# A graph network on one core: GpSimd clears a tile between its scatters, VectorE keeps small operands in PSUM, ScalarE makes source one-hots before it waits for flips

## What is computed

```python
gate = silu(edge_attr @ F1W + F1b) @ F2W + F2b
gate = gate + (ei * (ej @ adapt)).sum(-1, keepdims=True)   # kinds of the edge's two nodes
msg = gate * h[dst] * (cw * mj)[:, None]
agg = segment_sum(msg, src, num_segments=N)
for i in range(4):                                          # attention
    score = (qi * kj).sum(-1) + 0.1 * (edge_attr * qi[:, :RBF]).sum(-1) + logm[dst]
    ...
for _ in range(5):                                          # spreading
    h = (1.0 - ALPHA) * segment_sum(w[:, None] * h[row], col, num_segments=n) + ALPHA * x
```

## Time and profile before

| | |
|---|---|
| median of 3 runs | 8893.94 us (8884.61 to 8922.17) |
| the profiled execution | 8923.99 us, its span 8922.2 us |
| TensorE busy | 6968.6 us (78%) |
| VectorE busy | 5923.4 us (66%) |
| ScalarE busy | 4708.0 us (53%) |
| GpSimd busy | 5514.9 us (62%) in 7877 instructions |
| mean granted clock of TensorE | 0.874 of full speed |

### The profile page before, as it was taken

One profiled execution on the slowest core, in us unless ns is written; L12 is line 12 of the kernel. 1 busy time (PEld: TensorE's weight loads), 2 busy tenths in 40 slices (PEclk: granted clock), 3 DMA queues, 4 the chain that ended last, 5 costly groups with the idle time before them and its releaser, 6 DMA issues. The chain is left out here.

```text
span 8922.2 us, 298973 instructions
## 1 busy us (share of the span) xinstructions
PE 6968.6 (78%) x145656; PEld 6141.4 (69%) x92274; DVE 5923.4 (66%) x15778; ACT 4708.0 (53%) x14842; POOL 5514.9 (62%) x7877
## 2 busy tenths in 40 slices
PE   5544445444545999999699989998999989997998
PEld 4433333333334989988488858886888778887998
DVE  5555555555555889988688868886788678873111
ACT  0222222222223777777488858886788768881000
POOL 2266666666665666666488858886788768880000
PEclk9866666666667999999799979998999889998999
DMA  9522222222223777777377737773677457764565
GB/s 391 205 73 74 76 78 74 74 77 77 76 76 114 242 249 243 247 243 243 107 234 234 233 102 231 237 233 115 225 235 234 161 175 234 237 196 190 242 254 209
DMA packets 735833, 1616.82 MB, mean 181 GB/s; under 512 B 97576, under 2 KB 427272, under 8 KB 729955
## 3 DMA queue, kind: packets, MB, share of 16 engines
q1 hardware_dynamic: 674798, 1514.15, 50.6%
q0 software_dynamic: 52768, 77.90, 2.7%
q10 hardware_dynamic: 6869, 5.50, 0.2%
HBM read 1177.09 MB, written 420.09 MB: 179 GB/s over the span
## 5 line engine op out<-in xcount | busy, mean ns | idle before, releaser
L2011 ACT ACTIVATE vals<-carry_h,weight 128x49 f32<-128x49 f32 x9604 | 2322.8, 328 | 6.5
L1012 POOL DMA_INDIRECT edge_records<-rec_space,slot_all x1600 | 1587.5, 992 | 1104.4 <-DVE slot_all L995 560.2
L436 PE MATMUL psum<-TT,hd_t 128*128 128x97 bf16 x9604 | 1379.2, 208 | 106.0 <-POOL ts L2127 69.1
L430 PE MATMUL psum<-TT,hd_t 128*128 128x97 bf16 x19208 | 1443.4, 208 | 0.0
L436 PEld LDWEIGHTS psum<-TT,hd_t 128*128 128x128 fp8e4 x9604 | 938.2, 98 | 404.2 <-DVE carry_h L2125 69.9
L2056 POOL TENSOR_TENSOR vals<-vals 128x343 f32<-128x343 f32 x1372 | 1077.7, 785 | 92.8
L2051 POOL TENSOR_TENSOR vals<-vals 128x343 f32<-128x343 f32 x1372 | 1045.1, 762 | 4.6 <-ACT vals L2011 4.6
L771 ACT COPY attr_t<-psum 80x500 f32<-80x500 f32 x200 | 114.4, 572 | 1629.0 <-remote 1406.6
L430 PE MATMUL psum<-ts,hs_t 128*128 128x49 bf16 x19208 | 921.5, 184 | 0.1
L1916 DVE SCALAR_TENSOR_TENSOR xks<-recs,psum 128x343 f32<-128x343 f32 x1372 | 695.3, 507 | 331.5 <-PE psum L430 324.0
L1888 PE MATMUL psum<-vals,hs 128*128 128x147 bf16 x9604 | 873.0, 234 | 24.0 <-POOL vals L2056 24.0
(11 more groups left out here) (361 smaller groups left out, 15618.2 us busy)
## 6 DMA issues: line engine op xcount, KB each, us to landing
AJ<-adjacency SPq DMA_DIRECT2D x35, 5488.0 KB, 16.8
recs<-attributes SPq DMA_DIRECT2D x196, 686.0 KB, 5.5
hs<-one_hots SPq DMA_DIRECT2D x392, 336.0 KB, 3.1
one_hots<-hots SPq DMA_DIRECT2D x343, 336.0 KB, 4.1
edge_records<-zeros SPq DMA_DIRECT2D x49, 2278.5 KB
recs_g<-edge_records SPq DMA_DIRECT2D x343, 325.5 KB, 5.1
recs<-attributes SPq DMA_DIRECT2D x196, 514.5 KB, 3.7
hd_t<-one_hots SPq DMA_DIRECT2D x196, 448.0 KB, 4.7
```

What stands on the lines that cost most here:

```text
L430: return e.add_instruction(mybir.InstMatmult(name=nc.get_next_instruction_name(), engine=mybir.EngineType.PE, ldweights=False, start_tenso ...
L436: e.matmul(out, hot, parts[0], start=True, stop=False)
L1012: e.indirect_dma_start(REC[:, :], bass.IndirectOffsetOnAxis(ap=slot_all[:, i % SR, s:s + 1], axis=0), rec_rings[:, (i // 2) % 4, s, i % 2, ...
L2011: last = e.activation(vals[:, c, 0, :], carry_h[:, par(back), c, :], ACT.Copy, scale=weight[:, par(back), c:c + 1])
```

## The change

- `pause`, a new tile of 128 x 8 floats: ahead of the 2nd to the 8th scatter of an iteration GpSimd clears it (`memset`), raises the new semaphore `s_pause` and waits for it before the scatter.
- `iota_ps` (iota for the one-hots), `own_keys` (the keys of 25 steps, copied anew every 25, `KEYED`), `rank`, `slot_m` and `over_b` (the result of L990, until now written over `slot_b`) lie in PSUM bank 4 beside the mask. `told` gives the values of `s_load`, which now has some more steps: the copy of iota, and the 8 copies of keys, each with a wait for VectorE's step before.
- ScalarE calls `mark_sources(i + 2)` ahead of `take(i + 4)`.
- The semaphore `k_flat` is merged into `s_kept`, so that waits for the key rows also await the kind table's store (counts go up by 18).

```diff
+KEYED = 25
 FIRST_LAID, LAID_GAP = 36, 3
...
-            rank = sb(st, "rank", [EP, 2, NS])
-            slot_a, slot_b, slot_m = (sb(st, n, [EP, NS]) for n in ("slot_a", "slot_b", "slot_m"))
+            slot_a, slot_b = (sb(st, n, [EP, NS]) for n in ("slot_a", "slot_b"))
+            pause = sb(st, "pause", [P, 8])
...
-                    e.wait_ge(k_flat, 1)
+                    e.wait_ge(s_kept, 1)
-                    e.copy(embT, bank(6)[0:G, 0:NELEM]).then_inc(k_flat, 1)
+                    e.copy(embT, bank(6)[0:G, 0:NELEM]).then_inc(s_kept, 1)
-                    e.copy(EMB[:, 0:G], bank(6)[0:NELEM, 0:G]).then_inc(k_flat, 1)
-                    e.wait_ge(k_flat, 2)
-                    e.dma_start(KINDS[:, :], EMB).then_inc(k_flat, 16)
+                    e.copy(EMB[:, 0:G], bank(6)[0:NELEM, 0:G]).then_inc(s_kept, 1)
+                    e.wait_ge(s_kept, 2)
+                    e.dma_start(KINDS[:, :], EMB).then_inc(s_kept, 16)
-                    e.wait_ge(k_flat, 18)
+                    e.wait_ge(s_kept, 19)
...
-                    e.wait_ge(s_kept, 1)
+                    e.wait_ge(s_kept, 19)
...
-                    e.wait_ge(s_kept, 1)
+                    e.wait_ge(s_kept, 19)
...
                 by_stream = lambda arr: arr[:, :].rearrange("p (s i) -> p s i", s=NS)
                 found_ps = bank(0, 2)
                 hist_ps = bank(3)[:, 0:8 * NB].rearrange("p (q s b) -> p q s b", q=4, s=2)
-                mask = bank(4)[0:EP, 0:EP]
+                mask, iota_ps = bank(4)[0:EP, 0:EP], bank(4)[0:EP, P:P + NB]
+                own_keys = bank(4)[0:EP, 192:192 + KEYED * NS].rearrange("p (s i) -> p s i", s=NS)
+                rank = bank(4)[0:EP, 400:400 + 2 * NS].rearrange("p (r s) -> p r s", r=2)
+                slot_m, over_b = bank(4)[0:EP, 432:432 + NS], bank(4)[0:EP, 448:448 + NS]
                 pair_of = lambda hots, i, q: hots[:, i % 3, 2 * q:2 * q + 2, :].rearrange("p s b -> p (s b)")
 
...
                     mark_sources(0)
                     mark_sources(1)
                     for i in range(ITER):
-                        mlp_step(i + LEAD, "take", READY)
                         if i + 2 < ITER:
                             mark_sources(i + 2)
+                        mlp_step(i + LEAD, "take", READY)
                         mlp_step(i + LEAD - 1, "activate", READY)
                         mlp_step(i + LEAD - 2, "assemble", READY)
 
                 if name == "vector":
-                    iota49 = iota_f[0:EP, 0:NB].unsqueeze(1).broadcast_to([EP, NS, NB])
+                    iota49 = iota_ps.unsqueeze(1).broadcast_to([EP, NS, NB])
 
                     def make_hots(i):
...
                         e.tensor_tensor(one_bd[:, i % 3], iota49, bdv, ALU.is_equal).then_inc(s_hot, 1)
 
                     def rank_stream(i, s):
+                        if s == 0 and i % KEYED == 0:
+                            e.tensor_copy(own_keys, by_stream(key_f)[:, :, i:i + KEYED]).then_inc(s_load, 1)
+                            e.wait_ge(s_load, told(i - 1, 0) if i else 3)
                         if s == 0 and i % KC == 0:
                             e.wait_ge(s_keys[i // KC % 2], 16 * (i // KC // 2 + 1))
                         o = (i % KC) * NS * EP + s * EP
-                        last = e.scalar_tensor_tensor(junk[:, s * EP:(s + 1) * EP], key_rows[:, i // KC % 2, o:o + EP], key_f[:, s * SC + i:s * SC + i + 1], mask,
+                        last = e.scalar_tensor_tensor(junk[:, s * EP:(s + 1) * EP], key_rows[:, i // KC % 2, o:o + EP], own_keys[:, s, i % KEYED:i % KEYED + 1], mask,
                                                       ALU.is_equal, ALU.mult, accum_out=rank[:, i % 2, s:s + 1])
                         if s == NS - 1:
                             last.then_inc(s_rank, 1)
 
+                    told = lambda i, n: 3 + 4 * i + min(i + 1, ITER - 1) // KEYED + n
                     e.tensor_copy(mask, lower[:, :]).then_inc(s_load, 1)
+                    e.tensor_copy(iota_ps, iota_f[0:EP, 0:NB]).then_inc(s_load, 1)
+                    e.wait_ge(s_load, 2)
                     make_hots(0)
                     make_hots(1)
...
                     for s in range(2):
                         e.tensor_copy(next_base[64 * s:64 * s + NB, :, s, 1, :], base[64 * s:64 * s + NB, :, s, 1, :])
                     move_on(0)
-                    e.wait_ge(s_load, 1)
                     for s in range(NS):
                         rank_stream(0, s)
...
                         e.wait_ge(s_looked, i + 1)
                         e.tensor_reduce(found[:, :, :], look[:, :, :, :], AX.X, ALU.add).then_inc(s_load, 1)
                         rank_more(2)
-                        e.wait_ge(s_load, 4 * i + 2)
-                        e.tensor_tensor(slot_m[:, :], rank[:, i % 2, :], found[:, :, 0], ALU.add).then_inc(s_load, 1)
+                        e.wait_ge(s_load, told(i, 1))
+                        e.tensor_tensor(slot_m, rank[:, i % 2, :], found[:, :, 0], ALU.add).then_inc(s_load, 1)
                         rank_more(1)
-                        e.wait_ge(s_load, 4 * i + 3)
-                        e.scalar_tensor_tensor(slot_a[:, :], slot_m[:, :], float(NB), home[:, i % 3, :], ALU.mult, ALU.add)
-                        e.scalar_tensor_tensor(slot_b[:, :], slot_m[:, :], float(1 - NB), found[:, :, 1], ALU.mult, ALU.add).then_inc(s_load, 1)
+                        e.wait_ge(s_load, told(i, 2))
+                        e.scalar_tensor_tensor(slot_a[:, :], slot_m, float(NB), home[:, i % 3, :], ALU.mult, ALU.add)
+                        e.scalar_tensor_tensor(slot_b[:, :], slot_m, float(1 - NB), found[:, :, 1], ALU.mult, ALU.add).then_inc(s_load, 1)
                         rank_more(1)
-                        e.wait_ge(s_load, 4 * i + 4)
-                        e.scalar_tensor_tensor(slot_b[:, :], slot_m[:, :], float(CAP), slot_b[:, :], ALU.is_ge, ALU.mult).then_inc(s_load, 1)
+                        e.wait_ge(s_load, told(i, 3))
+                        e.scalar_tensor_tensor(over_b, slot_m, float(CAP), slot_b[:, :], ALU.is_ge, ALU.mult).then_inc(s_load, 1)
                         rank_more(2)
                         if i >= SR:
                             scattered(i - SR)
-                        e.wait_ge(s_load, 4 * i + 5)
-                        e.tensor_tensor(slot_i[:, i % SR, :], slot_a[:, :], slot_b[:, :], ALU.add).then_inc(s_idx, 1)
+                        e.wait_ge(s_load, told(i, 4))
+                        e.tensor_tensor(slot_i[:, i % SR, :], slot_a[:, :], over_b, ALU.add).then_inc(s_idx, 1)
                         if i + 1 < ITER - 1:
                             move_on(i + 1)
...
                         if i >= 4:
                             scattered(i - 4)
                         for s in range(NS):
+                            if s:
+                                e.memset(pause[:, :], 0.0).then_inc(s_pause, 1)
+                                e.wait_ge(s_pause, i * (NS - 1) + s)
                             e.indirect_dma_start(REC[:, :], bass.IndirectOffsetOnAxis(ap=slot_all[:, i % SR, s:s + 1], axis=0),
                                                  rec_rings[:, (i // 2) % 4, s, i % 2, :], None).then_inc(s_scat[i % 4], 16)
                     for i in range(ITER - 4, ITER):
```

More of the change, by code:

```diff
@@ L80, in build @@
         s_flat, s_found, s_looked = sem("place_cells_counted"), sem("place_bases_found"), sem("place_bases_looked_up")
-        s_kept, s_keys = sem("rows_in_dram"), [sem(f"key_rows_loaded_{k}") for k in range(2)]
+        s_kept, s_keys = sem("kinds_and_rows_in_dram"), [sem(f"key_rows_loaded_{k}") for k in range(2)]
         s_srcrows = [sem(f"source_rows_loaded_{k}") for k in range(2)]
@@ L89, in build @@
         s_apes, s_afold = sem("adj_multiplied"), sem("adj_folded")
[L90 removed]
+        s_kinds, k_taken, k_row = (sem("kinds_" + n) for n in ("loaded", "taken", "in_rows"))
+        s_pause = sem("place_pause_over")
         s_mixed, s_high, s_second, s_parts = (sem(n) for n in ("nodes_mixed", "node_high_parts", "node_low_parts", "node_parts_done"))
```

9 lines of the change are left out of this document (4 added, 5 removed).

## The result

The kernel before: 8910.3 us, median of five runs (8884.6 to 8922.2). The changed kernel: 8989.8 us, median of five (8961.4 to 9002.9). The ratio is 1.0087, with an interval of 1.0071 to 1.0102: the change makes the kernel 0.9% slower, by 79.5 us. The forecast was 8776 us, in a range of 8670 to 9040. The profiled execution of the changed kernel took 9002.9 us (span 9000.9), 78.9 us over that of before.

The account below looks back on a forecast made before the run. The edge placing was taken as bound by GpSimd and its waits on held-up semaphore updates. Scatters 1552, plain steps 61, pause steps 692 and waits 20 made 2325 against 2443 us: -118, 8776 us, range 8670 to 9040.

Parts of the forecast that it names:

- The step with a pause: Scatter end to next scatter's start on GpSimd with a clearing between: 0.49 us where 0.305 are now, bounds 0.36 and 0.70.
- (a): Time from a scatter's end to the start of the clearing on GpSimd: 0.10 us, bounds -0.04 and 0.30.
- The floor: If a pause were too short, GpSimd would await its own update longer, so steps are at least 0.39 to 0.44 us.
- the rival of 8658 us: The clearing overlaps the scatter's tail; steps held at 0.41 us, stage 2207 us, -236 us; chance 0.12.
- A pause that adds 0.19 us is more than either: The added pause exceeds the hold-up per scatter, 0.14 us from one GpSimd stop and 0.09 from the gathers.
- everyone was let go within a microsecond: In the placing, waiting engines went on within a microsecond of GpSimd's next start at 1487.74, after it ran dry.
- The second of its signs of being wrong: The prediction is wrong if VectorE still waits for its own results while GpSimd pauses.
- The waits: GpSimd's waits for VectorE's slot numbers in the placing: 20 us left where 396 were.
- The others' 6.7 us an iteration: Without hold-up VectorE needs 6.7 us an iteration of the placing against GpSimd's 11.5.
- The balance at a step of 0.58: Pause cost and gain balance at a 0.58 us step between scatters, given in the dearer-pause rival, chance 0.17.
- The hold-up is in the path, not in the row: Scatters' updates need on average what they take now, 12.2 us an iteration; pauses only move waits: 8894 us, chance 0.13.
- The pauses don't do what they say: The waits come from something else and stay: +231 us, 9125 us, chance 0.08.

Follow-up runs that it names:

- the table: Six kernels compared with the kernel before in sittings with hold-up: no pauses and five clearing sizes, steps 0.305 to 0.578 us; ratios 0.9931 to 1.0088.
- 0.465: Changed kernel with each pause clearing 88 elements instead of 8, with hold-up: stage 2450.6 us, waits 155 us, 1.0020 of the kernel before.
- 0.504: Changed kernel with each pause clearing 136 elements of 16 bits, with hold-up: stage 2384.6 us, waits 39 us, 0.9954 of the kernel before.
- a step of 0.578: Changed kernel with each pause clearing 224 elements of 16 bits, with hold-up: 8940.0 us, 1.0042 of the kernel before, stage 2454.4 us.
- the kernel with one of eight: Only the first of eight scatters an iteration issued, no pauses, in a sitting with hold-up, run once: 7921.9 us, stage 1418.8 us.

## Why the prediction was wrong

By its own steps, against the forecast stage of 2325 us and the measured 2512.

**The step with a pause: 0.494 expected, 0.397 measured.** Of its three terms the clearing (0.117; 0.119) and the time from it to the scatter (0.28; 0.278) were right. The term that failed is (a): I had split the 0.305 us between scatters into a tail of 0.10 us, in which the clearing couldn't start, and the rest. The clearing starts at the scatter's end: 0.00 us, inside the bounds of -0.04 to 0.30. With 1400 steps that made the pauses 136 us cheaper than forecast, less 22 us for the sixteen long steps, which no row of before let one foresee. The kernel should have gained by that; instead the pause became too short for its purpose: it adds 0.09 us, and by the prediction's own measure, 0.14 us of hold-up for each scatter, that is too little. By the table this decided the sign. Between the rows of the table for 0.465 and 0.504, a step of 0.494 would give a stage of about 2400 us (an estimate from these two rows), some 40 us under before.

**The floor: false, and it was to have caught just this.** "If it were too short, GpSimd would wait for its own update a little longer" was the safeguard of the forecast, and the basis of the rival of 8658 us. The two timelines around 1013 us show GpSimd's update through in 0.28 us while VectorE's is held for over 2, and of the 1400 steps with a clearing only the sixteen are longer than 0.50 us.

**The size and the kind of the hold-up.** "A pause that adds 0.19 us is more than either" rested on 0.14 us a scatter, from one stop of GpSimd, and 0.09 from the gather of kinds. By the table an added 0.09 does next to nothing for GpSimd's waits, 0.16 takes away half, 0.20 nearly all. All the waits of the stage over all its scatters, 368/1600 = 0.23 us for each, would have been a larger and more careful figure than that of one stop, but the fault is in the kind of sum: no figure per scatter gives this course. By 0.23 an added 0.09 us would leave 239 us of waits, where 314 were measured, and an added 0.20 us 88, where 39 were. And a stop doesn't let the updates through at once. The place that the earlier trace rows show has one more row:

```profile
1485.42 0.17 DVE L995 TENSOR_TENSOR slot_all<-slot_a,slot_b 125x8 int32<-125x8 f32 x1 [1.50 <-remote]
```

GpSimd ran dry at 1485.20, L995 ended at 1485.59, and the scatter that waits for it started at 1487.74, after 2.15 us in which GpSimd made nothing. L986 and L990, on the other hand, went on at 1480.39 and 1483.23, in the middle of the row of scatters, so the prediction's "everyone was let go within a microsecond" of GpSimd's next start is true of L771 alone among the three lines that it names. The second of its signs of being wrong came true, VectorE waiting for its own results while GpSimd pauses.

**The waits: 20 expected, 314 left.** This follows from the terms above. The sum missed by 187 us: +294 of waits, +7 of scatters (1559.5 for 1552), and -114 for the cheaper pauses (578 for 692, long steps included).

**Had the pause been what I took it for.** The kernel with a step of 0.504 is the one to ask: its stage is 2384.6, 59 us under before and not 118. The difference to 2325 is accounted for: 13 us for the longer step, 22 for the long steps, 19 for waits (39 and not 20), 6 for the scatters (1558 for 1552). The sum was thus right within 60 us at a dose that the change doesn't have. But most of the gain there isn't that of the pauses: the kernel without any has a stage of 2366.8.

**What was right.** The PSUM operands: 28 us of shorter scatters in the changed kernel, 40 without pauses in the sitting without hold-up, for a forecast of 35; no scatter of the changed kernel over 0.998 us. The rule of the Trainium skill (SBUF — State Buffer, "Who interferes with whom") on two SBUF inputs is borne out by that. The order and the merged semaphores at 0 (1.0014 and 1.0015 measured, at the edge of what can be told from nothing). The others' 6.7 us an iteration (7.1 on the average). The balance at a step of 0.58.

**The rivals.** "The hold-up is in the path, not in the row" had come nearest: pauses too short for their purpose mostly move waits, and the stage comes out between 2367 and 2512 in the six kernels of the table. I gave it 0.13 because in the earlier trace rows two iterations took 22.6 us, 11.3 each, against 12.2 on the average; from start to start (1464.62 to 1487.74) they took 23.1, or 11.6 each, since some of those scatters were long, and it was one place against the sum of all. But its strict form is false: a fixed time per update would leave the stage alike, and it ranged over 145 us; and with a step of 0.578 hardly any hold-up was left. "The pauses don't do what they say" was expected at 9125 us with all the waits left and a step of 0.494; with the true step of 0.397 the same reasoning gives 2443 + 1400 x 0.092 + 22 - 28 = 2566, 54 us more than measured. So that rival, with the right length, is close to what happened in the changed kernel. It leaned on the Trainium skill (SBUF — State Buffer, "Who interferes with whom"), by which TensorE and ScalarE never wait on anyone. That section speaks of SBUF ports, while ScalarE's idle time here is waiting for late semaphore updates of TensorE. So the prediction went too far in saying that these idle times speak against the rule; the rule says nothing of them.

**What stays open.** What brings or takes the hold-up between sittings isn't known; by their times all runs of the kernel before in a sitting had it or none had (8876 to 8930 us, or 8538 to 8569). Nor is what the held updates wait for inside the chip: that it depends on GpSimd's scatters is shown by the kernel with one of eight (no hold-up at all) and by the dose, but not whether their making or their transfers do it, nor the place where the updates queue. A step between 0.504 and 0.518, at which GpSimd's own time alone would still be under the 2367 us of the kernel without pauses, wasn't run; by these rows it could gain 20 us of stage at most (an estimate). The sixteen long steps come with the clearings in every kernel that has 1400 of them, with and without hold-up; their cause wasn't tried.

**The better kernel.** The changed kernel without its pauses is faster than the kernel before in each of the three sittings in which it was run: 0.9956, 0.9957 and, with hold-up, 0.9931 of its time, 8852.1 us against 8903.9. With hold-up it is also faster than the changed kernel (1.0087).

## What to carry to other kernels

A pause on the engine that bounds a stage has to bring more than it costs, and its dose decides: here the first 0.09 us took away almost none of GpSimd's waits and the next 0.11 almost all, so run at least three lengths before keeping one. Judge the cure by the engines that were held up and not by the one that is being slowed: with a step of 0.504 GpSimd had stopped waiting, and the others were still held. Take the size of a stall from all of its waits over the whole stage and not from the one place where the timeline shows it best, and don't trust a sum in proportion before two lengths have borne it out. And ask in how many sittings the stall is there at all, for a cure is paid for in those without it as well (1.8% here), while a change that shortens the bounding engine's own work, such as the operands in PSUM, paid in all of them.

## What the runs showed of the hardware that I had not expected

- In some sittings the semaphore updates of TensorE and VectorE come late while GpSimd issues indirect DMAs one every 1.28 to 1.48 us: in the changed kernel up to 32 us after the end of TensorE's instruction and up to 5.8 us after VectorE's. At one every 1.56 us (0.977 + 0.578) 76 of TensorE's 720 recorded updates were over 1 us late and none of VectorE's. Updates of GpSimd and ScalarE are on time all the while; ScalarE idles because it waits for TensorE's. In other sittings the same kernel shows none of it: the stage of the kernel with the order alone is 2078.1 us there and 2426.9 here, the whole kernel 8562 and 8911.
- A clearing on GpSimd may start at the very end of an indirect DMA, although the next indirect DMA needs 0.305 us; and a small clearing costs 0.118 us for 8 elements of 32 bits, 0.153 for 48, 0.186 for 88, and 0.225 and 0.299 for 136 and 224 of 16 bits.
- Writing a sum read from VectorE's accumulator takes 142 ns each into PSUM (80 into SBUF, in the kernel before), 1584 of them 225 us; VectorE had that time to spare. It was within the 0.1 us an instruction that the prediction allowed.
